# A routed feed-forward block whose down projection becomes three products of rounded pieces

## The reference, cut to what matters

```
x = layernorm(x + conv(x) * x)                 # a decaying complex recurrence along the 32 sequences
x = layernorm(x + attention(x, ctx))           # 16 heads of 16 channels, projections, softmax
# third layer, for each token, with the expert e nearest to its normed row xn (8 experts)
h = xn @ up_w[e]                               # 256 -> 1024
a, g = split(h)                                # 512 and 512
y = (a * silu(g)) @ down_w[e]                  # 512 -> 256, "the down projection"
x = layernorm(x + (y + x))
```

## Time and profile before

| | |
|---|---|
| median of 3 runs | 1206.01 us (1204.95 to 1211.37) |
| the profiled execution: its own time, its span | 1200.62 us, 1198.9 us |
| first stage | about 0 to 808 us |
| second stage, first down projection to last | 820.6 to 1188 us, 71 tiles |
| busy in 1000 to 1100 us | PE 100.0, PEld 83.7, DVE 55.8, ACT 28.8, POOL 36.3 us |
| DMA in the same stretch | 0.48 of 16 engines, 148 GB/s |

### The profile page before, as it was taken

One profiled execution on the slowest core, in us unless ns is written; L12 is line 12 of the kernel. 1 busy time (PEld: TensorE's weight loads), 2 busy tenths in 40 slices (PEclk: granted clock), 3 DMA queues, 4 the chain that ended last, 5 costly groups with the idle time before them and its releaser, 6 DMA issues.

```text
span 1198.9 us, 27888 instructions
## 1 busy us (share of the span) xinstructions
PE 1109.3 (93%) x8314; PEld 826.7 (69%) x8315; DVE 959.3 (80%) x2437; ACT 668.3 (56%) x1417; POOL 770.7 (64%) x933
## 2 busy tenths in 40 slices
PE   4999999999998999999999999989999999999996
PEld 3776666666666666666666666658788888888885
DVE  6569999999999999999999999887755555555553
ACT  4267777777776777777777777763222222222221
POOL 4747878888987998898889883255333333333333
PEclk9999999999999999999999999989999999999998
DMA  5767677766655656655656545213554444445442
GB/s 119 194 172 211 188 183 192 194 158 154 153 147 137 159 148 148 168 146 150 156 142 159 149 126 121 52 28 116 176 155 150 151 148 147 155 150 156 146 149 88
DMA packets 124097, 178.04 MB, mean 149 GB/s; under 512 B 13670, under 2 KB 111599, under 8 KB 117776
## 3 DMA queue, kind: packets, MB, share of 16 engines
q1 hardware_dynamic: 117456, 159.65, 50.4%
q0 software_dynamic: 6528, 16.99, 4.7%
HBM read 124.47 MB, written 53.03 MB: 148 GB/s over the span
## 4 chain that ended last, share of the span: by engine, by line
PE 39%; DVE 35%; issue 10%; POOL 7%; DMA 5%; SPq 2%; ACT 2%; POOLq 0%; DVEq 0%; ACTq 0%
DVE neg_max_sb L1556 14%; PE Y L488 10%; PE G L450 8%; PE A L450 8%; DVE oq L1755 4%; DVE u L1574 4%; PE GT L460 2%; POOL buckets L849 2%; POOL state L805 2%; DMA neg_max<-nm_row 2%; PE M L1186 2%; PE S L1229 2%; DVE stx L1540 2%; DVE st L1540 2%; DVE row L1663 1%
## 5 line engine op out<-in xcount | busy, mean ns | idle before, releaser
L1556 DVE TENSOR_REDUCE neg_max_sb<-S 128x2 f32<-128x512 f32 x512 | 327.5, 681 | 33.0 <-PE S L1229 32.4
L1019 ACT ACTIVATE probs<-T 128x512 f32<-128x512 f32 x512 | 278.1, 595 | 135.7 <-PE T L1242 121.0
L1229 PE MATMUL S<-k_st,q_st 48*128 48x256 f32 x1024 | 208.1, 311 | 32.7 <-DVE neg_max_sb L1556 30.2
L1229 PEld LDWEIGHTS S<-k_st,q_st 48*128 48x128 f32 x1024 | 140.8, 185 | 102.6 <-issue 69.8
L1242 PE MATMUL T<-q_st,k_st 49*128 49x256 f32 x1024 | 204.4, 311 | 5.6 <-DMA q_st<-neg_max 2.3
L428 ACT ACTIVATE gT<-GT 128x512 f32<-128x512 f32 x71 | 42.5, 598 | 205.4 <-PE GT L460 202.1
L1242 PEld LDWEIGHTS T<-q_st,k_st 49*128 49x128 f32 x1024 | 140.8, 185 | 20.6 <-ACT probs L1019 13.2
L408 POOL DMA_INDIRECT out<-res,token x71 | 76.0, 1071 | 102.0 <-DVE res L575 97.0
L1178 PE MATMUL O<-probs,v_aug 128*32 128x256 f32 x2048 | 139.7, 391 | 0.7 <-ACT probs L1019 0.7
L488 PE MATMUL Y<-dn_sb,gT 128*128 128x256 f32 x568 | 134.5, 379 | 1.5 <-DMA dn_sb<-in_L_ffn_down_w 0.8
L849 POOL DMA_INDIRECT buckets<-row,slot x64 | 67.1, 1049 | 84.4 <-DVE slot L1810 73.5
(11 more groups left out here) (212 smaller groups left out, 2587.9 us busy)
## 6 DMA issues: line engine op xcount, KB each, us to landing
dn_sb<-in_L_ffn_down_w SPq DMA_DIRECT2D x71, 512.0 KB
k_st<-k_pieces SPq DMA_DIRECT2D x64, 256.0 KB, 3.7
q_st<-q_pieces SPq DMA_DIRECT2D x64, 256.0 KB, 3.7
xr<-buckets SPq DMA_DIRECT2D x71, 129.0 KB
xt<-in_x SPq DMA_DIRECT2D x32, 256.0 KB, 6.4
ct<-in_ctx SPq DMA_DIRECT2D x32, 256.0 KB, 6.8
k_pieces<-k_hi SPq DMA_DIRECT2D x32, 256.0 KB
k_pieces<-k_lo SPq DMA_DIRECT2D x32, 256.0 KB
```

What stands on the lines that cost most here:

```text
L1019: a_.activation(probs[:, h % 8].rearrange("p k t -> p (k t)"), T_ps[h % 2][:, :], ACT.Exp, scale=DH ** -0.5).then_inc(s["exp_ok"], 1)
L1229: last = t_.matmul(S_ps[h % 2][:, c * TOK:(c + 1) * TOK], q_st[h // HPC][base:base + STACK, h % HPC, c * P:(c + 1) * P], k_st[h // HPC][ba ...
L1556: v.tensor_reduce(neg_max[:, cur.mod(2), :, h], S_ps[h % 2][:, :].rearrange("p (c t) -> p c t", c=NTC), AX.X, ALU.max, negate=True).then_i ...
```

## The change

Each expert's down weights are cut once into an upper piece `hi` and a lower piece `lo` (float32r each) and kept in a new DRAM tensor `down_pieces` with one row of 8 KB for each expert and partition. The cut is made in the first stage in `up_sb`, which is free there: SP loads the eight experts' down weights at the start (8 loads of 512 KB), ACT rounds them (`upper_down`) in step 0, DVE subtracts (`lower_down`) in steps 0 and 1, and SP writes both pieces back (`store_down`) in steps 1 to 8. The loads of the up weights come after that, in steps 9 to 25, as 32 loads of 256 KB with rows of 2 KB. In the second stage SP loads 1 MB per tile instead of 512 KB, DVE makes a lower piece of `gT` ahead of `res`, and PE makes 12 float32r products per tile instead of 4 float32 ones. `gated` is written in place of `gate`, `picked` in place of `past`, and small tensors move to other free places; `gT` holds two pieces of one tile instead of one piece of two tiles, and so its copy on ACT waits for the down projection of one tile before, not of two.

```diff
-UP_STEPS = (0, 1, 2, 3, 4, 5, 6, 7)
+DOWN_STEPS = (1, 2, 3, 4, 5, 6, 7, 8)
+FIRST_UP = 9
+UP_STEPS = 17
+UP_PARTS = 4
+DOWN_HI_AT = {(0, h): (k,) for k, h in enumerate((1, 2, 4, 6, 8, 9, 10, 11))}
+DOWN_LO_AT = {(0, 7): (0,), (0, 9): (1,), (0, 15): (2,), (1, 1): (3,), (1, 5): (4,), (1, 7): (5,), (1, 9): (6,), (1, 11): (7,)}
...
-            gated = sb2("gated", [P, HID])
-            gT = sb2("gT", [P, 2, HCH * P])
-            dn_sb = sb2("dn_sb", [P, 2, DNW])
+            gated = gate
+            gT = sb2("gT", [P, 2, HCH * P], F32R)
+            dn_sb = sb2("dn_sb", [P, 2, 2, DNW], F32R)
...
-                        wait(act, "y_pe", m - 2)
-                        a_.activation(gT[:, m.mod(2)], GT_ps[:, :], ACT.Copy).then_inc(z["gT_ok"], 1)
+                        wait(act, "y_pe", m - 1)
+                        a_.activation(gT[:, 0], GT_ps[:, :], ACT.Copy).then_inc(z["gT_ok"], 1)
...
-                        wait(pe, "gT_ok", m - 1)
+                        wait(pe, "gT_lo", m - 1)
...
-                        wait(pe, "gT_ok", m)
+                        wait(pe, "gT_lo", m)
...
-                        for c in range(HCH):
-                            last = t_.matmul(Y_ps[:, 0:C], gT[:, m.mod(2), c * P:(c + 1) * P], dn_sb[:, m.mod(2), c * C:(c + 1) * C],
-                                             start=(c == 0), stop=(c == HCH - 1))
+                        terms = [(w, d, c) for c in range(HCH) for w, d in ((0, 0), (0, 1), (1, 0))]
+                        for k, (w, d, c) in enumerate(terms):
+                            last = t_.matmul(Y_ps[:, 0:C], gT[:, w, c * P:(c + 1) * P], dn_sb[:, m.mod(2), d, c * C:(c + 1) * C],
+                                             start=(k == 0), stop=(k == len(terms) - 1))
...
+                    if active(m):
+                        wait(dve, "gT_ok", m)
+                        v.tensor_tensor(gT[:, 1], GT_ps[:, :], gT[:, 0].bitcast(F32), ALU.subtract).then_inc(z["gT_lo"], 1)
...
+                def store_down(e, w):
+
+                    sp.wait_ge(s["down_lo"], e + 1)
+                    at = slice(((1 - w) * E + e) * DNW, ((1 - w) * E + e + 1) * DNW)
+                    sp.dma_start(down_dram[e, :, w * DNW:(w + 1) * DNW], up_sb[:, at].bitcast(F32)).then_inc(s["down_out"], 16)
...
+                    if t.k in DOWN_STEPS:
+                        store_down(DOWN_STEPS.index(t.k), 0)
+                    if FIRST_UP <= t.k < FIRST_UP + UP_STEPS:
+                        ups(t.k - FIRST_UP)
                     read_q(nxt, 1)
                     read_k(nxt, 1)
-
-                    if t.k in UP_STEPS:
-                        ups(UP_STEPS.index(t.k))
+                    if t.k in DOWN_STEPS:
+                        store_down(DOWN_STEPS.index(t.k), 1)
...
+                def upper_down(e):
+
+                    if e == 0:
+                        act.wait_ge(s["down_in"], 16 * E)
+                    a_.activation(up_sb[:, (E + e) * DNW:(E + e + 1) * DNW], up_sb[:, e * DNW:(e + 1) * DNW].bitcast(F32), ACT.Copy)\
+                        .then_inc(s["down_hi"], 1)
...
+                def lower_down(e):
+
+                    dve.wait_ge(s["down_hi"], e + 1)
+                    at, hi = slice(e * DNW, (e + 1) * DNW), slice((E + e) * DNW, (E + e + 1) * DNW)
+                    v.tensor_tensor(up_sb[:, at], up_sb[:, at].bitcast(F32), up_sb[:, hi].bitcast(F32), ALU.subtract).then_inc(s["down_lo"], 1)
```

More of the change, by code:

```diff
@@ L283, in experts @@
             xr = sb2("xr", [P, RING, ROWW])
+            xsT = sb2("xsT", [P, 2, 2, NCH * P], F32R)
+            gate = sb2("gate", [P, HID])
+            gated = gate
+            gT = sb2("gT", [P, 2, HCH * P], F32R)
+            res = sb2("res", [P, 2, C])
+            dn_sb = sb2("dn_sb", [P, 2, 2, DNW], F32R)
+            old = HPC * TOK + 8 * NTC * TOK + 4 * NTC * (H * VW + 32 - VW)
+            sb2("beside_v", [P, old - RING * ROWW - 4 * NCH * P - HID - 2 * HCH * P - 2 * C - 4 * DNW])
             xs = sb2("xs", [P, C])
@@ L307, in experts, with sb_small @@
-            rs3 = sb2("rs3", [P, 2])
-            token = sb2("token", [P, 2], U32)
+            small = [0]
+            def sb_small(name, shape, dt=F32):
+                n = 1
+                for d in shape[1:]:
+                    n *= d
+                small[0] += (n + 7) // 8 * 8
+                return sb2(name, [P] + shape[1:], dt)[0:shape[0]]
+            count = sb_small("count", [1, E])
+            tiles, ends = scan[:, 0, E:2 * E], scan[:, 1, E:2 * E]
+            full = sb_small("full", [1, E])
@@ new lines, in experts @@
+            skip = sb_small("skip", [1, E])
+            owned = sb_small("owned", [1, MAIN])
+            row_f = sb_small("row_f", [1, 2, NTILES])
+            eno_f = sb_small("eno_f", [1, NTILES])
+            past_e = sb_small("past_early", [1, EARLY, E])
+            picked_e = past_e
+            st3 = sb_small("st3", [P, 6])
+            mv3 = sb_small("mv3", [P, 2])
+            rs3 = sb_small("rs3", [P, 2])
+            token = sb_small("token", [P, 2], U32)
+            sb2("beside_x1", [P, 2 * NTC * C - 2 * C - small[0] + 2 * NTC * C])
@@ L687, in _ @@
                 sp.dma_start(cent, centroids).then_inc(s["params"], 16)
+                for e in range(E):
+                    dst = up_sb[:, e * DNW:(e + 1) * DNW].bitcast(F32).rearrange("p (o n) -> p o n", o=HCH)
+                    sp.dma_start(dst, down_w[e].rearrange("(o p) n -> p o n", p=P)).then_inc(s["down_in"], 16)
                 def write_keys(item):
@@ L695, in write_keys, with ups @@
                     write_piece(item, k_dram, 1, k_lo, k_out)
[L697 to L700 removed]
+                def store_down(e, w):
+                    sp.wait_ge(s["down_lo"], e + 1)
+                    at = slice(((1 - w) * E + e) * DNW, ((1 - w) * E + e + 1) * DNW)
+                    sp.dma_start(down_dram[e, :, w * DNW:(w + 1) * DNW], up_sb[:, at].bitcast(F32)).then_inc(s["down_out"], 16)
+                def ups(k):
+                    if k == 0:
+                        sp.wait_ge(s["down_out"], 2 * 16 * E)
+                    for part in range(k * E * UP_PARTS // UP_STEPS, (k + 1) * E * UP_PARTS // UP_STEPS):
+                        e, n = part // UP_PARTS, UPW // UP_PARTS
+                        row, col = divmod(part % UP_PARTS * n, 2 * HID)
+                        at = part * n
+                        sp.dma_start(up_sb[:, at:at + n].bitcast(F32), up_w[e, row * P:(row + 1) * P, col:col + n]).then_inc(s["ups"], 16)
                 def step(t):
@@ L1127, in step @@
                             copy_sums(prv, 0)
+                        for e in DOWN_HI_AT.get((t.k, h), ()):
+                            upper_down(e)
                         for e in HI_AT.get((t.k, h), ()):
```

41 lines of the change are left out of this document (13 added, 28 removed).

## The result

The changed kernel took 1219.09 us (median of 5 runs, 1214.28 to 1221.14), the kernel before 1206.01 (5 runs). The ratio is 1.0098, 95% interval 1.0072 to 1.0124: about 1% slower, where 1197 us and "faster" were predicted, and outside the range of 1184 to 1211. The profiled execution took 1214.28 us with a span of 1212.5, 13.6 more than the span before.

A forecast was written before the change was run, and what follows sets the result against it. PE was taken to bound the second stage; the first had no single bound. Terms of -20.6, +3, +2.2, +1, +3.5 and +2.2 summed to -8.7 us, taking 1206.0 to 1197 us, range 1184 to 1211.

The forecast's parts named there:

- The new P is 4.81: Second stage, PE's product: period from 5.16 to 4.81 us, 0.35 less per tile, 20.6 us gained over 59 tiles.
- So P = 4.81 stands for DVE too: Second stage, DVE: its chain with the added lower piece of gT also fits a period of 4.81 us.
- The waits for loads: Second stage, 1 MB down loads: landing in 4.9 us, a quarter of 59 tiles wait 0.19 us, +3 us.
- rival (b): Second stage: landing in 5.35 us makes the load half bound the loop, P 5.01, 1202 to 1207 us; chance 0.18.
- The first 12 tiles: Overlap of the stages: exposed gT piece and longer down loads in tiles 7 to 11, +2.2 us with the last tile.
- Start: First stage's start: eight 512 KB down loads delay x, context and the first scores, +1 us, from 0 to 4.
- passes: Steps 0 and 1: ACT's roundings free, DVE's eight subtractions 0.45 us each unabsorbed, +3.5 us, bounds 0 and +18.
- traffic: First stage, DMA: stores cost as today's loads, moved up loads in steps 9 to 25 add +2.2 us, -2 to +5.
- the piece of gT: Second stage, DVE: 0.69 us between moments and `res`, fitting while DVE waits for POOL; cost 0 per usual tile.
- (c): Second stage: 1 MB landing in 5.9 us bounds the loop outright, P 5.29, 1225 us; chance 0.05.
- (d): Steps 0 and 1: DVE and POOL exclude each other, all eight subtractions +2.3 us, 1212 us; chance 0.09.
- (e): Second stage: weight loads pace PE's product, twelve matmuls take 2.27 us, P 5.7, 1247 us; chance 0.04.

The follow-up runs named there:

- e1_early_index: Changed kernel with PE's read of the tile's index moved ahead of its wait for the gated tile: 1215.74 us, ratio 1.0069 to the kernel before.
- e3_both: Changed kernel with the early index read and only the upper 512 KB of each down load (lower weights left out of the result): 1199.25 us, ratio 0.9912.
- e5_stage1_only: Changed kernel's first stage and buffers with the kernel before's down projection; pieces made and stored, not used: 1222.81 us, ratio 1.0123.
- e17_stage1_again: Changed kernel's first stage with the old down projection, pieces stored but unused, same file timed a second time: 1215.37 us, ratio 1.0103.
- e12_before_late_ups: Kernel before with only the up weights' loads moved, 32 of 256 KB in steps 9 to 25, no pieces or stores: 1205.89 us, ratio 0.9990.
- e14_pieces_no_stores: Changed kernel's first stage with the old down projection, pieces made but their 16 stores left out: 1209.09 us, ratio 1.0048.
- e18_smooth: Changed kernel with early index and row-number reads, four places for down pieces, tiles 11 to 14 loaded in steps 11 and 12: 1200.28 us, ratio 0.9983.
- e6_act_loads: Changed kernel with the early index read and down loads issued on ScalarE's queue behind its copy of GT: 1255.24 us, ratio 1.0369.
- experiment 1: Index read moved ahead of the wait for the gated tile, in the changed kernel (1215.74 us, 1.0069) and the kernel before (1205.24 us, 0.9972).
- e10_early_reads: Changed kernel with the early index read, and SyncE reading both row numbers ahead of its wait for the token copy: 1207.16 us, ratio 1.0002.

## Why the prediction was wrong

**The step that failed** is "The new P is 4.81", and with it "So P = 4.81 stands for DVE too". It was summed from PE's records alone. Two things were off in it. The smaller is the size of one record, 0.120 instead of 0.115 us: P by PE is 4.88 (0.30 a tile won, not 0.35), 59 x 0.05 = 3 us. The larger is that something else stands between GT and G: the read of the index in TensorE's own queue, behind the wait for the gated tile. What covered it was the time from the gate's end (1002.82) to GT (1003.60). The trace before has it, and the sum did not look at it. It shows no time in the table of waits there, since nothing waited. After, it costs 0.21 us in nearly every period and makes 5.09 of 4.88, 13.5 us in the loop if nothing else hides it.

**The waits for loads.** +3 was predicted, by a landing time of 4.9 us; it was 5.1 at the median. The 4.0 that they cost in the loop (296.0 against 292.0 with half loads) look like a hit, but that is luck. The sum had a quarter of the tiles wait 0.19 us each. In the trace one load of 7.36 us made 3.2 of the 4.0, partly through the slower clock behind it, and the other 55 periods have 0.8 in all, because the late index gives each load 0.4 us more per two periods. At the period of 4.88 us, for which the term was meant, the same loads cost 11.6 (`e1_early_index` against `e3_both`), four times the term. That is the mechanism of rival (b), the load half bounds the loop. Its P of 5.01 would make a loop of 285.6 us; the one of `e1_early_index` is 290.1, and its 1215.74 us lie above the rival's 1202 to 1207.

**The first 12 tiles.** +2.2 predicted, +6.5 measured. The place is right, the size not: the two loads in the chain there took 6.67 and 6.33 us, where 4.47 and 3.93 had stood and the sum had added 1.44 to each. From the chain after:

```profile
859.70 6.67 DMA dn_sb<-down_pieces
866.42 2.93 PE Y L508 x12
...
879.60 6.33 DMA dn_sb<-down_pieces
885.97 1.69 PE Y L508 x12
```

With half loads the twelve took 69.5 instead of 74.2, so most of the 6.5 is the load. The padding, the table's work and the rows stand in the same queue, and a likely reading is that the second half megabyte therefore costs more than its share of a free queue; no run tests it. The sum also lacked the clock: TensorE did nothing from 864.0 to 866.0, and Y behind the first of the two loads took 2.93 us at a granted clock of 0.50, 1.5 more than 1.44. Before, the clock stayed at 1.00 through both waits, and Y took 2.01 and 1.99 us behind them.

```profile
864.00:866.00 2.00, 0.00 (x0) 0.00 (x0) 1.21 (x3) 0.00 (x0) 0.92 (x1) 1.00 0.71 217
866.40:869.30 2.90, 2.88 (x13) 2.88 (x14) 0.49 (x1) 0.00 (x0) 0.00 (x0) 0.50 0.78 290
```

**The first stage.** Start +1, passes +3.5 and traffic +2.2 made 6.7; the profiled executions differ by 6.6, and the medians of the changed kernel leave 6 for it. But the same first stage alone (`e5_stage1_only`, `e17_stage1_again`) cost 12 to 17, and its parts, measured there, are not those of the sum; so the total is at best a hit by luck, and the spread stays open. The passes may be right: +3.2 at the median, though from nothing to 5 is possible, with VectorE's subtractions at 1.21 to 2.33 us, median 1.75, for the 1.23 + 0.45 of the sum. The start costs some 3 instead of 1. The traffic term was mis-sized, and it was put on the wrong part: the up loads moved to steps 9 to 25 cost nothing (`e12_before_late_ups`), the stores, which were taken to be "as costly as today's loads" and so free, cost about 6 (`e17_stage1_again` over `e14_pieces_no_stores`). VectorE's passes in the trace after (count, ns min/median/max, first and last start):

```profile
L1707 DVE TENSOR_TENSOR up_sb<-up_sb x8: 1210/1750/2332, 53.3 to 82.3; 128x1024 fp32r<-128x1024 f32 x8
```

**What was right**: twelve Y records in 1.44 us (1.38 predicted), the piece of gT in POOL's shadow at no cost, a gain of PE's that comes out one for one when nothing else is late (`e3_both`: -17.0 in the loop), and rivals (c), (d) and (e) not happening.

**VectorE and GpSimd.** The rule of the Trainium skill ("SBUF — State Buffer", Who interferes with whom) is that a VectorE instruction with two SBUF inputs and a GpSimd one that reads SBUF exclude each other for a whole instruction. The trace after agrees. The two subtractions with nothing on POOL beside them took 1.22 us; one more, at 82.27, took 1.21, and POOL's product beside it 3.36 instead of 2.36. The five others lasted until about 1.1 us after the POOL instruction that they had met, as here:

```profile
55.86 1.27 POOL L838 TENSOR_TENSOR state<-state,by_re 128x512 f32<-128x512 f32 x1
55.88 2.33 DVE L1707 TENSOR_TENSOR up_sb<-up_sb 128x1024 fp32r<-128x1024 f32 x1
57.28 2.06 POOL L845 TENSOR_TENSOR state<-state,xt 128x512 f32<-128x512 f32 x1
```

POOL's product ends at 57.13, the subtraction 1.09 later at 58.22, and POOL's next one, which began at 57.28, 1.1 after that. Rival (d) did not fail because the two engines share without waiting, but because the POOL instructions met here take 1.27 us, not the 2.35 of `by_re` in the earlier trace rows by which (d) was priced. A wait of 1.1 us at most and none in three of eight gives the median of 1.75. The row of `x` in the earlier trace rows, with which the prediction found the rule agreed, has one full tensor and two columns as sources, so it bears on the rule less directly than these rows.

**The sum as it came out**, for the profiled executions: first stage +6.6, first 12 tiles +6.5, loop -17.0 + 13.5 + 4.0 = +0.5, together 13.6. The +4.0 and a part of the +6.5 hold some 3 us of slower clock behind long waits. The medians lie 5.4 (before) and 4.8 us (after) above these executions.

**A version faster than both** was not found. `e18_smooth` is level with the kernel before (0.9983, 0.9960 to 1.0007) and 1% or so under the changed one: its loop wins 16.6 us, its first 12 tiles lose 5 and its first stage 10 or so. `e3_both` is faster (0.9912) but leaves out the weights' lower piece.

## What to carry to other kernels

When a product is shortened, list what every engine's queue does between its waits, register reads too, and ask for each how much cover it has and whether the shortening takes it: a cost that shows no wait today has no row in the table of waits. Two costs that hide in each other can't be read off one at a time; take both away once, and then each alone. When a term comes out near its forecast, look whether it is made up as the sum had it: here a term of 3 was met by one late load. And before a load is issued earlier, ask what it goes ahead of: with a megabyte in front of a small load that stands in a circle of waits, `e6_act_loads` lost 3.7%.

## What the runs showed of the hardware

- A register read in TensorE's queue took 0.30 us (rows of experiment 1), but what depends on it started 1.0 us after the wait ahead of it ended (1003.14 to 1004.15).
- The 512 KB loads at the start held SyncE's queue: the eight issues stand from 11.5 to 21.5 us and take 0.40 to 2.45 us each, where an issue is 0.24 to 0.5 in the later rows of this queue.
- Loads of 1 MB in rows of 8 KB landed in 5.1 us at the median with xr ahead of them, in single cases in 7.36 (trace after, 916.22) and 7.76 us (`e10_early_reads`).
- A float32r product of 256 columns took 0.120 us with its own weight load of 128 columns, twelve in a row.
- TensorE's granted clock fell from 1.00 to 0.50 at 866.4 and 924.4 in the trace after. It had done nothing from 864.0 to 866.0 and from 922.0 to 923.6, waiting for a load. Y's twelve products took 2.93 and 2.27 us there instead of 1.44.
- Five VectorE subtractions with two sources in SBUF ended about 1.1 us after the POOL instruction beside them; alone they took 1.22 us.
- The same first stage takes 10 us more or less from one execution to the next, with a mean granted clock of 0.979 in the longer profile and 0.986 in the shorter. The changed kernel's and its relatives' executions range over 12 us and more, so no single profile gives its cost.
